# An early-fusion transformer block on one core: 32-bit saturating y hats, 16-bit scores in key pairs, and a new order of turns

## The reference: what is computed

```python
h = leaky_relu(batchnorm(conv2d(x, stem_w, stem_b, 4)))        # 96 x 21 x 21
offset = conv2d(h, off_w, off_b, 4)                            # 16 taps, 25 positions, y and x
py = base_y + kh + off[..., 0, :, :]; px = base_x + kw + off[..., 1, :, :]
sampled = v00*(1-wy)*(1-wx) + v01*(1-wy)*wx + v10*wy*(1-wx) + v11*wy*wx
h = concatenate([tokens(leaky_relu(bn2(dcn(sampled)))), txt])  # 25 + 77 = 102 tokens of 192

attn = fake_quant(q @ k * sc, s_attn)                          # 12 heads, clipped to -128..127
x_int = attn / scale; x_int = x_int - max(x_int)
x_int = maximum(x_int, 30 * x0_int)
qq = floor(x_int / x0_int); r = x_int - x0_int * qq
exp_int = maximum(floor((r * (r + b_int) + c_int) * 2.0 ** (30 - qq)), 0)
ratio = round(sum(exp_int) / maximum(exp_int, 1))              # then a power of two from log2(ratio)
h = h + fake_quant(o @ wp.T + b_proj, s_act3)
h = h + gelu(layernorm(h) @ w_in.T + b_in) @ w_out
```

## Times and profile before

| what | value |
|---|---|
| time, median of 3 runs | 1013.89 us (1013.72 to 1017.25) |
| span of the profiled execution | 1014.5 us |
| a time of the profiled execution apart from its span | the page gives none |
| PE, DVE, ACT, POOL busy over the span | 87%, 86%, 77%, 26% |
| granted TensorE clock, mean over the span | 0.951 |

### The profile page before, as it was taken

One profiled execution on the slowest core, in us unless ns is written; L12 is line 12 of the kernel. 1 busy time (PEld: TensorE's weight loads), 2 busy tenths in 40 slices (PEclk: granted clock), 3 DMA queues, 4 the chain that ended last, 5 costly groups with the idle time before them and its releaser, 6 DMA issues. The chain is left out here.

```text
span 1014.5 us, 18281 instructions
## 1 busy us (share of the span) xinstructions
PE 880.8 (87%) x5594; PEld 539.9 (53%) x5594; DVE 876.0 (86%) x1695; ACT 779.8 (77%) x1529; POOL 266.9 (26%) x248
## 2 busy tenths in 40 slices
...
## 3 DMA queue, kind: packets, MB, share of 16 engines
...
## 5 line engine op out<-in xcount | busy, mean ns | idle before, releaser
L563 POOL TENSOR_TENSOR ee_sb<-ee_sb,rs_sb 128x1020 f32<-128x1020 f32 x64 | 157.2, 2464 | 379.1 <-DVE rs_sb L1059 379.1
L1195 PE MATMUL bank<-hats_sb,ht_sb 127*96 127x400 f32 (+1 forms) x384 | 147.9, 522 | 1.7 <-DVE hats_sb L921 1.7
L1327 PE MATMUL bank<-w_out_sb,ge_sb 128*102 128x192 f32 x768 | 138.8, 331 | 10.9 <-DVE y_sb L1096 6.9
L1327 PEld LDWEIGHTS bank<-w_out_sb,ge_sb 128*102 128x102 f32 x768 | 120.3, 168 | 31.6 <-issue 17.8
L921 DVE TENSOR_TENSOR hats_sb<-hats_sb 126x1600 f32<-126x1600 f32 x64 | 127.2, 1987 | 0.7
L648 ACT ACTIVATE hats_sb<-bank 126x400 f32<-126x400 f32 (+1 forms) x256 | 108.2, 523 | 0.3 <-PE bank L1181 0.3
L727 ACT ACTIVATE a_sb<-scores,sc_sb 128x1020 f16<-128x1020 f32 x64 | 71.1, 1111 | 39.2 <-PE scores L1279 39.2
L1195 PEld LDWEIGHTS bank<-hats_sb,ht_sb 127*96 127x96 f32 (+1 forms) x384 | 58.7, 166 | 72.6 <-issue 69.3
L734 ACT ACTIVATE sq_sb<-rm_sb,sc_sb 128x1020 f32<-128x1020 f16 x64 | 73.5, 1148 | 18.2 <-DVE rm_sb L1031 18.0
L572 POOL TENSOR_TENSOR xshift_sb<-mv_sb,xshift_sb 102x4 f32<-102x4 f32 (+1 forms) x33 | 11.0, 333 | 279.9 <-DVE ve_sb L961 278.5
L1242 PE MATMUL bank<-xt_sb,w_in_sb 128*128 128x408 f32 (+1 forms) x204 | 82.0, 527 | 1.0 <-ACT xt_sb L667 1.0
...
## 6 DMA issues: line engine op xcount, KB each, us to landing
...
q_sb<-qb_sb SPq DMA_DIRECT2D x192, 12.8 KB, 1.9
samp_sb<-samp_sb SPq DMA_DIRECT2D x48, 50.0 KB, 1.9
...
```

The source lines that it names most:

```text
L563: nc.gpsimd.tensor_tensor(EE[b][:], EE[b][:], RS[b][:].unsqueeze(2).to_broadcast([128, RT, TOK]), ALU.mult).then_inc(scaled_done, 1)
L1195: last = mm(dst, HT[0:rows, t.i, j, :], HATS[t.i][0:rows, 1 + j, :], start=(j == 0 and not odd), stop=(j == NCH - 2 and odd == 1))
L1327: last = mm(bank[t.banks[0]][0:TOK, 0:D], GE[:, f, t.i * TOK:(t.i + 1) * TOK], WOUT[:, f, :], start=(f == 0), stop=(f == FT - 1))
```

## The change

1. **Saturating y hats.** ACT writes the four y parts as 32-bit integers, |dy| times 2^31; the conversion clips at the largest integer, which is what min(|dy|, 1) would give. So DVE's HAT treats only the x part (400 elements in place of 2000), and HATW becomes a scalar_tensor_tensor of 1600 elements that subtracts 2^31 and multiplies. HAT no longer waits for the y parts; HATW does.
2. **16-bit integer scores in key pairs.** The free dimension of the scores is laid out as 51 key pairs x 10 rows x 2 keys, in place of 10 rows x 102 keys. PE writes the scores in that order (51 runs of 2 in a bank), ACT writes `A16` as int16. A new DVE stage CLP clips them once, at the front; the clip in DST and the stage BND go. DST becomes a tensor_tensor of three int16 tensors, with the minimum held twice per row so that it can be read in pairs. QQ, QQG, REM and EP work on int16. SUM and MXC read their rows in pairs with a hop between them; PR on ACT reads in pairs and writes rows. NRM on POOL reads the reciprocals in pairs.
3. **A new table of turns and new banks.** All entries of SLOT and most of BANKS are replaced. Five more one-column constants are computed at the start.

```diff
-dve.MXB.54 act.XH2.17 pe.INT.9 dve.QQG.55 act.XH2.16 dve.MXC.54 pe.PV3.16 act.V.12 dve.REM.55
...
+dve.FF2.57 act.LN2X.17 pe.LN2X.20 dve.SUM.52 act.SQ.14 dve.RCP.52 pe.SC.16 act.OFS.4 dve.PR.54
...
-BANKS = dict(FFA=(1, 0, 4, 2), STEM0=(5, 4), STEM1=(0, 4), HTT=(5,), OFF=(1,), OFS=(0,), HAT=(5, 0),
-             INT=(3, 2), DCN=(4,), LN1X=(2,), LN2X=(0,), V0=(4, 1), V1=(4, 3), FQ0=(5, 2),
-             FQ1=(0, 4), PV2=(1,), PV3=(4,), FFN0=(5, 3), FFN1=(0, 1), FFN2=(4, 2), FF2=(3,))
+BANKS = dict(FFA=(3, 2, 0, 1), STEM0=(0, 3), STEM1=(1, 5), HTT=(0,), OFF=(4,), OFS=(3,),
+             HAT=(0, 5), INT=(3, 4), DCN=(1,), LN1X=(4,), LN2X=(2,), V0=(1, 0), V1=(3, 5),
+             FQ0=(5, 3), FQ1=(4, 2), PV2=(1,), PV3=(2,), FFN0=(4, 5), FFN1=(2, 0), FFN2=(1, 3),
+             FF2=(2,))
...
+        def by_row(flat):
+            return flat.rearrange("p (k r e) -> p r k e", r=RT, e=2)
+        def over_key_pairs(rows):
+            return rows.rearrange("p r e -> p (r e)").unsqueeze(1).to_broadcast([128, KP, PAIRS])
...
-                nc.gpsimd.tensor_tensor(EE[b][:], EE[b][:], RS[b][:].unsqueeze(2).to_broadcast([128, RT, TOK]),
+                scaled = EE[b][:].rearrange("p (k q) -> p k q", q=PAIRS)
+                nc.gpsimd.tensor_tensor(scaled, scaled, over_key_pairs(RS[b][:]),
                                         ALU.mult).then_inc(scaled_done, 1)
...
-                    nc.scalar.activation(HATS[t.i][0:rows, 1 + j, :], bank[t.banks[1]][0:rows, 0:SMP], ACT.Abs,
-                                         bias=float(-line)).then_inc(ay_done, 1)
+                    nc.scalar.activation(HATS[t.i][0:rows, 1 + j, :].bitcast(i32), bank[t.banks[1]][0:rows, 0:SMP], ACT.Abs,
+                                         scale=ONE_Y, bias=-line * ONE_Y).then_inc(ay_done, 1)
...
-                nc.scalar.activation(A16[b][:].rearrange("p (j r) k -> p j (r k)", j=2), SCORES[:, :, 0:RC // 2], ACT.Identity,
-                                     scale=sc[:, SCORE:SCORE + 1], bias=MAGIC16).then_inc(a16_done, 1)
+                nc.scalar.activation(A16[b][:].rearrange("p (k j q) -> p j k q", j=2, q=RT),
+                                     SCORES[:, :, 0:RC // 2].rearrange("p j (k q) -> p j k q", q=RT), ACT.Identity,
+                                     scale=sc[:, SCORE:SCORE + 1], bias=EVEN_LIFT).then_inc(a16_done, 1)
...
-                v.tensor_scalar(hat, hat, -1.0, 0.0, ALU.add, ALU.min).then_inc(hat_done, 1)
+                v.tensor_scalar(hat, hat, -1.0 / ONE_Y, 0.0, ALU.add, ALU.min).then_inc(hat_done, 1)
...
-                v.tensor_tensor(hat[:, 1:, :], hat[:, 1:, :], hat[:, 0:1, :].to_broadcast([rows, NCH, SMP]),
-                                ALU.mult).then_inc(w_done, 1)
+                dve.wait_ge(ay_done, t.count(NCH, NCH))
+                v.scalar_tensor_tensor(hat[:, 1:, :], hat[:, 1:, :].bitcast(i32), -ONE_Y,
+                                       hat[:, 0:1, :].to_broadcast([rows, NCH, SMP]), ALU.add, ALU.mult).then_inc(w_done, 1)
...
+            def clip(t):
+                a = A16[t.i % 2][:]
+                dve.wait_ge(a16_done, t.count(1, 1))
+                v.tensor_scalar(a, a, EVEN_LIFT - 127.0, EVEN_LIFT + 128.0, ALU.max, ALU.min).then_inc(clip_done, 1)
...
-                v.scalar_tensor_tensor(M16[b][:], A16[b][:], MAGIC16 + 128.0, MX[b][:].unsqueeze(2).to_broadcast([128, RT, TOK]),
-                                       ALU.min, ALU.subtract).then_inc(m_done, 1)
-            def bound(t):
-                v.tensor_scalar(M16[b][:], M16[b][:], 0.0, sc[:, G30:G30 + 1], ALU.max, ALU.min).then_inc(mc_done, 1)
+                v.tensor_tensor(M16[b][:].rearrange("p (k q) -> p k q", q=PAIRS), A16[b][:].rearrange("p (k q) -> p k q", q=PAIRS),
+                                over_key_pairs(MX[b][:]),
+                                ALU.subtract).then_inc(m_done, 1)
...
-                v.tensor_reduce(SS[b][:], EE[b][:], AX.X, ALU.add).then_inc(ss_done, 1)
+                v.tensor_reduce(SS[b][:], by_row(EE[b][:]), AX.XY, ALU.add).then_inc(ss_done, 1)
...
-                    dst = SCORES[:, r // (RT // 2), r % (RT // 2) * TOK:(r % (RT // 2) + 1) * TOK]
+                    dst = SCORES[:, r // RB, 0:KP * RT].rearrange("p (k r e) -> p r k e", r=RB, e=2)[:, r % RB, :, :]
```

More of the change, by code:

```diff
@@ L78 @@
-pe.SC.13 dve.MXB.52 act.FFN0.16 dve.DST.53 act.FFN1.16 pe.OFF.4 dve.BND.53 act.FFN2.16 sp.YO0.20
-dve.RCP.54 pe.LN2X.17 pool.NRM.16 act.STEM.3 dve.QQ.53 dve.LS1.51 act.LOG.14 pe.DCN.8 dve.LS1.50
-act.SQ.13 dve.LS1.49 pe.LN2X.16 act.HAT.7 dve.LS1.48 dve.LN1.48 act.STEM.2 pe.SC.12 dve.VE1.48
-sp.SD.8 act.XH1.11 dve.QQG.53 pe.OFS.4 act.PR.14 dve.REM.53 act.HTT.4 pe.FFA.16 dve.MXC.52 dve.PW.55
-pool.RS2A.16 act.XH1.10 pe.FFN0.16 dve.EP.53 act.LN1X.11 dve.DST.52 act.SQ.12 pe.FFN1.16 dve.FF2.59
-sp.LX.0 dve.BND.52 act.XH1.9 pe.FFN2.16 dve.PR.55 act.LN1X.10 dve.QQ.52 act.PV2.15 pe.STEM0.0
@@ L84 @@
-dve.EXP.53 act.XH1.8 dve.QQG.52 pe.FF2.19 dve.EP.52 act.HAT.6 dve.FF2.58 pe.HAT.7 act.OC.15
-pool.RS2.16 sp.LR.12 dve.REM.52 act.LN1X.9 dve.PW.54 pe.FF2.18 dve.SUM.53 act.V.11 dve.HAT.47
-pe.HTT.4 act.LOG.13 dve.RCP.53 act.LN1X.8 dve.EXP.52 pe.LN1X.11 act.PR.13 dve.FF2.57 sp.DCN.8
-dve.SUM.52 pe.FF2.17 act.LOG.12 dve.RCP.52 act.V.10 dve.PR.54 pe.HAT.6 act.PR.12 pool.NRM.15
-dve.FF2.56 dve.HATW.47 pe.LN1X.10 act.FQ0.8 dve.PW.53 act.PV2.14 pe.PV2.15 dve.PR.53 act.FQ1.8
-sp.LA.8 dve.PV3.55 pe.LN1X.9 act.OC.14 dve.RES.55 dve.PW.52 act.HAT.5 pe.V0.8 dve.PR.52 act.HAT.4
@@ new lines @@
+pe.FF2.20 dve.MXB.51 dve.MXC.51 pool.NRM.25 act.XH1.8 pe.LN1X.12 dve.DST.51 act.STEM.2 dve.CLP.50
+act.LOG.13 pe.PV3.19 dve.QQ.51 sp.LA.40 dve.MAX.50 act.LN1X.8 pe.FQ0.12 dve.QQG.51 act.PR.13
+dve.MXB.50 act.LOG.12 pe.PV2.18 dve.REM.51 act.V.11 dve.MXC.50 pe.FQ1.12 dve.EP.51 act.PR.12
+dve.DST.50 act.V.10 pe.HAT.9 pool.NRM.24 sp.YO1.52 dve.EXP.51 act.FQ0.8 dve.PREP3.44 pe.INT.11
+dve.QQ.50 act.FQ1.8 dve.SUM.51 pe.PV2.17 act.PV2.14 dve.EP.50 act.HAT.5 dve.QQG.50 pe.HAT.8
+act.OC.14 dve.CLP.49 sp.LX.32 dve.REM.50 pe.PV3.18 act.PV2.13 dve.MAX.49 act.OC.13 dve.RCP.51
@@ new lines @@
+pe.INT.10 act.INT.7 pool.RS2A.24 dve.PREP1.16 dve.MXB.49 pe.PV3.17 act.HAT.4 dve.MXC.49 act.HTT.3
+pe.PV2.16 dve.EXP.50 act.PV2.12 sp.RP.36 dve.DST.49 pe.HTT.7 act.OC.12 dve.CLP.48 dve.QQ.49
+act.INT.6 pe.INT.9 dve.SUM.50 act.SC.11 dve.QQG.49 pe.PV3.16 act.VC.11 dve.MAX.48 dve.REM.49
+act.STEM.1 pool.RS2.24 pe.SC.15 dve.RCP.50 sp.PT.47 act.SC.10 dve.MXB.48 pe.STEM1.4 act.XH2.15
+dve.LS1.47 act.XH2.14 dve.LS1.46 pe.HTT.6 dve.LS1.45 act.INT.5 dve.LS1.44 pe.SC.14 act.STEM.0
+dve.LN1.44 act.HTT.2 dve.MXC.48 pe.INT.8 sp.LR.44 dve.EP.49 act.INT.4 dve.DST.48 pe.V1.12 act.SQ.11
```

131 lines of the change are left out of this document (70 added, 61 removed).

## The result

The changed kernel takes 1004.25 us (median of 4 runs, 996.3 to 1004.8), the kernel before on the same chip 1013.81 (1011.69 to 1017.25): ratio 0.9886, 95% interval [0.9848, 0.9924]. On another chip, 6 runs of the changed kernel gave 996.33 (993.45 to 1002.52), ratio 0.9847 [0.9814, 0.988]. So the change is faster by 1.1 to 1.5%. The forecast was 988, 2.5%.

The account below looks back on a forecast made before the run. DVE was taken to bound the kernel narrowly, then PE. From a span of 1014.5 us, 22.7 for fourteen rounds and 3.4 for the ends gave 988.4, forecast 988; own range 972 to 1000, with rivals 968 to 1010.

Parts of the forecast that it names:

- DVE sets the pace by a narrow margin: Middle rounds before: DVE busy 52.65 of 55.32 us and bounding, PE right behind at 52.50.
- now PE bounds, plus 1.2 idle: Rounds after: PE busy 52.5 us plus 1.2 idle makes 53.7, 1.6 less than 55.32.
- the forecast's own signs of being wrong: PE's busy time per round moving over 0.5, eleven score matmuls over 0.65 us, or PE idle staying above 2.
- The new order ... neither removes nor adds work; it decides whether 1.2 is 0.2 or 2.8.: Table of turns: claimed to affect only PE's idle time per round, taken as 1.2 us.
- DVE's 1361 ns per image: Summed DVE savings over HAT, HATW, DST, BND, CLP, QQ and small costs; 5.4 us per round, 52.65 to 47.2.
- the hats' weights: HATW on DVE: scalar_tensor_tensor for tensor_tensor, forecast to cost 30 ns more per image, from 0 to 86.
- the bound of 770: PR on ACT reading 510 pairs: at most 0.77 us, 3.1 per round; 0 was taken.
- writing the scores as 102 runs: ACT's score write in 102 runs of 10: forecast 150 ns more, 0.6 us per round.
- The scores in pairs: PE's score output in runs of 2: no change taken; rival that pairs slow PE, 1022 us, chance 0.08.
- 780.1 - 22.7: Fourteen rounds took 780.1 us before; 1.6 less per round was forecast to save 22.7.
- ends: Filling and draining: one HAT, 0.8 us, plus 2.6 from four images' softmax chains; together 3.4, from 0 to 6.
- PE stays 52.5: PE's busy time per round, forecast unchanged because the matmuls of a round stay.

Follow-up runs that it names:

- e4: The kernel before with the integer y hats alone, in its old order: 1021.6 us, ratio 1.0103.
- e16: The kernel before with the new hats and POOL's reciprocal-sum multiplication on 10 of 1020 columns: 1005.13 us (without the new hats 1006.31).
- e8: The changed kernel with the clip on 20 of the 1020 scores alone: 996.15 us, ratio 0.9836 to the kernel before.
- e6: The changed kernel without the last 2 of 6 hidden blocks of the second feed-forward product: 995.98 us, ratio 0.9847 to the kernel before.
- e2: All new operations with the kernel before's table of turns and banks: 1056.32 us, ratio 1.0422 to the kernel before.
- e5: The changed kernel with ACT's PR reading and writing in a row, DVE's PW reading the pairs: 1017.23 us, ratio 1.005 to the kernel before.
- e14: The changed kernel with pairs read by DVE's PW instead of ACT's PR, and POOL's four-column multiplication L591 on DVE: 995.25 us, ratio 0.9833.
- e13: The changed kernel with POOL's four-column multiplication L591 done by DVE: 996.03 us (994.03 to 1001.56).

## Why the prediction was wrong, by its steps

- **"DVE sets the pace by a narrow margin"** is the step that failed. It was read from busy shares of 95%, and from waits being short. Relieving DVE (e4, e16, e8) gained 0.2 us per round at most, relieving PE (e6) nothing. With it fell "now PE bounds, plus 1.2 idle". The middle round came out at 53.77 against 53.7 forecast, but not for the reason given; that is luck: the same sum would have forecast a gain for e4 and e2, which lost 1 and 4%. Two of the forecast's own signs of being wrong did show: PE's busy time moved by 1.2 us (limit 0.5), and PE idles 2.5 us in a round (limit 2, 1.2 forecast). What the runs show in its place is a round that no engine's busy time sets (best 53.4 to 53.5, with PE at 49.1 to 51.3 and DVE at 47.2 to 49.1), and hold-ups between POOL and DVE that can take back what cheaper operations save (22 us in e5, the larger part of 43 in e2). What does set 53.4 stays open.
- **"The new order ... neither removes nor adds work; it decides whether 1.2 is 0.2 or 2.8."** It decided far more: 4.2% to -1.5% for the same operations.
- **DVE's 1361 ns per image**: HAT 463 and 368 (forecast 430), DST 722 (692), clip 456 (419), sum unchanged. Half of the hats' weights were misread: rows 5 show the form with 127 rows, 1824 ns; the other took longer, since 14 of its 32 had met POOL's multiplication.

```profile
L921 DVE TENSOR_TENSOR hats_sb<-hats_sb 126x1600 f32<-126x1600 f32 x32 | 68.8, 2151 | 0.1
```

  With 1822 and 1817 after, the weights gave 168 ns per image in the mean where -30 was forecast; the middle step of the minimum (MXB, 419 to 260) gave 159 more. Missing on the other side: L1025 at 716 ns (+493), held by POOL, the step behind the ratio at 540 where it took 438, exp +62, reciprocal +60. DVE's whole saving was 65.6 / 64 = 1.03 us per image, 4.3 per round instead of 5.4.
- **ACT**: 48.55 per round against 48.7, by luck: the pairs cost 210 ns where 0 was taken (the bound of 770 held), and writing the scores as 102 runs cost 6 (1117 against 1111) where 150 was taken. In time the pairs show nothing: e14, without them, is no faster than e13 (0.9833 against 0.9846, intervals overlapping).
- **The scores in pairs**: 212 ns per matmul against 215, and the median eleven take 0.76 us from the first start to the last end in both kernels. Here the rule of the Trainium skill that the forecast cites ("SBUF — State Buffer", "Door 1: The DMA port swizzle"), that any non-contiguous access to PSUM slows matmuls, doesn't hold for float32 results written two side by side.
- **From 988 to 1004.** In the profiled execution: fourteen rounds of 760.4 us where 780.1 - 22.7 = 757.4 was forecast (3.0 more), ends -0.6 where -3.4 was taken, and the time of a run 2.1 above its span where 0.6 below was taken: 988.4 + 3.0 + 2.8 + 2.1 = 996.3. The other three runs on that chip stood 8 us higher; on the second chip the median was 996.3. That 8 is not explained, and it is half of the 16 us between 988 and 1004.
- **"PE stays 52.5"**: it is busy for 51.29 us per round with the same number of matmuls. Their ends are modelled and depend on what follows, so a new order changes the figure; no run here turned that into time.
